# Attention's running maxima from row-packed scores: two half-array products of 64 rows in place of one of 96

## The reference, cut to what matters

```
scores = einsum('bhqd,bhkd->bhqk', q, k) / sqrt(16)      # masked by layer
attn   = softmax(scores)                                  # over the keys
out    = einsum('bhqk,bhkd->bhqd', attn, v)
```

## The kernel before, in words

| stage | max units | their matmuls, columns | score columns (L675, L678) | sum groups (L694) |
|---|---|---|---|---|
| layer 1, 8 tiles | 32 | 64, 25,616 | 26,624 | 26 |
| layer 2 | 48 | 106, 35,978 | 36,608 | 26 |
| layer 3 | 100 | 224, 90,144 | 92,160 | 58 |

## Time and profile before

### The profile page before, as it was taken

One profiled execution on the slowest core, in us unless ns is written; L12 is line 12 of the kernel. 1 busy time (PEld: TensorE's weight loads), 2 busy tenths in 40 slices (PEclk: granted clock), 3 DMA queues, 4 the chain that ended last, 5 costly groups with the idle time before them and its releaser, 6 DMA issues.

```text
span 5943.9 us, 71309 instructions
## 1 busy us (share of the span) xinstructions
PE 3795.9 (64%) x19888; PEld 1731.9 (29%) x19894; DVE 2791.6 (47%) x3817; ACT 1990.8 (33%) x3720; POOL 1506.2 (25%) x1461
## 2 busy tenths in 40 slices
PE   7700410037962013996599969974899999997695
PEld 2300200022321001332133336862222222222485
DVE  3131221276753276776566630013766666673201
ACT  1100100014751001673155621212366666664131
POOL 0767777677767400000000010010000000000202
PEclk9555655557986555998699979986799999999698
DMA  2331311013321211110211111534100111101243
GB/s 83 90 118 24 108 38 24 21 55 106 92 93 39 92 66 48 51 51 20 81 52 47 42 60 65 192 137 117 43 25 25 32 33 33 33 25 32 110 181 135
DMA packets 195461, 403.88 MB, mean 68 GB/s; under 512 B 46405, under 2 KB 130649, under 8 KB 186074
## 3 DMA queue, kind: packets, MB, share of 16 engines
q1 hardware_dynamic: 147114, 323.79, 17.0%
q0 software_dynamic: 48112, 77.16, 4.6%
HBM read 301.77 MB, written 106.10 MB: 69 GB/s over the span
## 4 chain that ended last, share of the span: by engine, by line
PE 47%; POOL 20%; DVE 10%; issue 10%; DMA 7%; ACT 2%; SPq 1%; POOLq 1%; DVEq 1%; ACTq 0%; PEldq 0%
POOL got_late L1319 13%; PE PS L694 13%; PE PS L657 9%; PE PS L675 8%; POOL s_got L1319 6%; PE PS L1959 5%; PE PS L1969 5%; DVE a_maxima L789 3%; ACT a_probs L745 1%; DMA q_parts<-a_parts 1%; PE PS L1929 1%; DMA late_rows<-got_late 1%; PE PS L1937 1%; PE PS L1122 1%; DMA Y<-denominators 1%
## 5 line engine op out<-in xcount | busy, mean ns | idle before, releaser
L789 DVE TENSOR_REDUCE a_maxima<-PS 128x1 f32<-128x1024 f32 (+8 forms) x1696 | 1637.9, 990 | 685.3 <-PE PS L657 468.7
L745 ACT ACTIVATE a_probs<-PS 128x512 f32<-128x512 f32 (+4 forms) x2896 | 1503.3, 572 | 771.7 <-PE PS L675 568.3
L657 PE MATMUL PS<-a_k_max,a_q_max 96*128 96x512 bf16 (+2 forms) x3136 | 913.5, 371 | 153.1 <-DVE a_maxima L789 90.4
L675 PE MATMUL PS<-a_q_exp,a_k_exp 97*128 97x512 bf16 (+4 forms) x2896 | 970.2, 376 | 58.6 <-ACT a_probs L745 30.6
L694 PE MATMUL PS<-a_probs,a_v_head 128*32 128x256 f32 (+4 forms) x7456 | 964.5, 496 | 31.8 <-DVE a_v_head L804 11.2
L2145 POOL IOTA e_slot_no<- 128x23 f32 x2 | 0.3, 162 | 2944.1 <-DVEq L2207 2944.1
L1319 POOL DMA_INDIRECT got_late<-kv_table,numbers x560 | 576.8, 1030 | 171.9 <-issue 171.9
L675 PEld LDWEIGHTS PS<-a_q_exp,a_k_exp 97*128 97x128 bf16 (+1 forms) x2896 | 271.7, 99 | 697.6 <-ACT a_probs L745 442.7
L657 PEld LDWEIGHTS PS<-a_k_max,a_q_max 96*128 96x128 bf16 x3136 | 263.8, 100 | 692.9 <-DVE a_maxima L789 386.6
L1319 POOL DMA_INDIRECT s_got<-kv_table,s_numbers x400 | 428.5, 1071 | 121.9 <-issue 121.9
L1298 PE MATMUL PS<-identity,s_ctx 128*128 128x128 f32 x18 | 6.2, 449 | 668.9 <-DVE s_ctx L1274 668.9
(11 more groups left out here) (342 smaller groups left out, 3309.9 us busy)
## 6 DMA issues: line engine op xcount, KB each, us to landing
e_w<-in_ew SPq DMA_DIRECT2D x41, 2052.0 KB, 8.1
late_rows<-got_late POOLq DMA_DIRECT2D x7, 2560.0 KB, 7.9
m_got<-late_rows SPq DMA_DIRECT2D x7, 2560.0 KB, 9.2
a_k_max<-k_parts SPq DMA_DIRECT2D x48, 300.2 KB, 3.8
a_k_exp<-k_parts SPq DMA_DIRECT2D x48, 300.2 KB
a_q_max<-q_parts SPq DMA_DIRECT2D x32, 384.0 KB, 3.6
a_q_exp<-q_parts SPq DMA_DIRECT2D x32, 384.0 KB
a_k_max<-k_parts SPq DMA_DIRECT2D x16, 684.2 KB, 5.7
```

Source lines behind the costliest of these rows:

```text
L657: last = pe.matmul(bank[:, b0:b1], q_max[hh][:, P * t:P * (t + 1)], k_max[hh][:, k0 + b0:k0 + b1], start=True, stop=not (lo < hi or masked))
L675: last = pe.matmul(bank[0:rows, q - CH * c:CH], k_exp[hh][:, k0:k0 + rows], q_exp[hh][:, q:CH * (c + 1)], start=True, stop=not (on_diag or ...
L745: act.activation(probs[i % PROB_SLOTS][0:rows, q - CH * c:CH], exp_bank[i % EXP_BANKS][0:rows, q - CH * c:CH], ACT.Exp).then_inc(probs_rea ...
L789: dve.tensor_reduce(maxima[hh][:, t, k0 // MAX_COLS:k0 // MAX_COLS + 1], max_bank[s[1] % MAX_SLOTS][:, 0:w], AX.X, ALU.max).then_inc(max_t ...
```

## The change

Four of the six groups of rows (64 rows) are used for the maxima. They stand first in DRAM, by a new order of the rows; the exponentials still use all 96. Two copies of the 64 query rows lie in partitions 0 to 63 and 64 to 127, and half of the keys beside each, so that a max unit is two matmuls of 64 rows, each in its own half of the array's rows and with its own PSUM bank. For causal keys the halves alternate every 256 keys. The diagonal's mask stays a matmul of 128 rows. Where the halves differ in width, VectorE makes two reductions of a unit. Layer 3's units don't cross from context to own keys any more. The row order now takes four stores for each piece in place of three, and `load_max` issues 4, 5 or 6 DMAs in place of two.

```diff
-QUERY_ROWS = ((0, 1, 2), (0, 1), (0,))
-KEY_ROWS = ((0, 0, 0), (1, 1), (2,))
+QUERY_ROWS = ((0, 1), (0, 1), (2,), (0,))
+KEY_ROWS = ((0, 0), (1, 1), (0,), (2,))
+HALF_ROWS = 4 * HD
+TURN = 256
+SPLIT_STORES = 16 * len(QUERY_ROWS)
...
+    sections = key_sections(n)
...
+                for c in range(0, lower, CH):
+                    wl, wu = min(CH, lower - c), max(0, min(CH, upper - c))
+                    max_steps.append(("max", len(max_units)))
+                    max_units.append((hh, t, at + c, wl, wu, slot, even, c, seen - P * t))
...
-                    for b0 in range(0, w, CH):
-                        b1 = min(b0 + CH, w)
-                        lo, hi = max(d0, k0 + b0), min(d1, k0 + b1)
-                        last = pe.matmul(bank[:, b0:b1], q_max[hh][:, P * t:P * (t + 1)], k_max[hh][:, k0 + b0:k0 + b1],
-                                         start=True, stop=not (lo < hi or masked))
...
+                    for half, w in enumerate((wl, wu)):
+                        if w:
+                            rows = slice(HALF_ROWS * half, HALF_ROWS * (half + 1))
+                            last = pe.matmul(bank[:, CH * half:CH * half + w], q_max[hh][rows, P * t:P * (t + 1)],
+                                             k_max[hh][rows, at:at + w], start=True,
+                                             stop=not (masked or (on_diag and d == half)))
+                    if on_diag:
+                        last = pe.matmul(bank[:, CH * d + d_at:CH * d + d_at + min(P, ahead)], env.mask_diag[:, :],
+                                         env.above_qk[:, 0:min(P, ahead)], start=False, stop=True)
...
-                    dve.tensor_reduce(maxima[hh][:, t, k0 // MAX_COLS:k0 // MAX_COLS + 1], max_bank[s[1] % MAX_SLOTS][:, 0:w],
-                                      AX.X, ALU.max).then_inc(max_taken, 1)
+                    if wu:
+                        taken = dve.tensor_reduce(maxima[hh][:, t, slot:slot + 1], bank.rearrange("p (b c) -> p b c", b=2)[:, :, 0:wu],
+                                                 AX.XY, ALU.max)
+                        slot += 1
+                    if wl > wu:
+                        taken = dve.tensor_reduce(maxima[hh][:, t, slot:slot + 1], bank[:, wu:wl], AX.X, ALU.max)
+                    taken.then_inc(max_taken, 1)
...
-            sp.dma_start(q_max[hh][:, :], head_rows(env.q_parts, h, T)).then_inc(q_max_in[hh], 16)
-            sp.dma_start(k_max[hh][:, :], head_rows(env.k_parts[n], h, keys)).then_inc(q_max_in[hh], 16)
+            whole = head_rows(env.k_parts[n], h, keys)
+            for half in range(2):
+                rows = slice(HALF_ROWS * half, HALF_ROWS * (half + 1))
+                sp.dma_start(q_max[hh][rows, :], head_rows(env.q_parts, h, T)[0:HALF_ROWS, :]).then_inc(q_max_in[hh], 16)
+                for even, at, base, length in sections:
+                    if even:
+                        w, first = (length + 1) // 2, base + (length - (length + 1) // 2) * half
+                        sp.dma_start(k_max[hh][rows, at:at + w], whole[0:HALF_ROWS, first:first + w]).then_inc(q_max_in[hh], 16)
+                        continue
...
+def key_sections(n):
+    even = (True, 0, 0, M)
+    return {1: [even], 2: [(False, 0, 0, M)], 3: [even, (False, (M + 3) // 4 * 2, M, S)]}[n]
+
+def half_columns(seen, half):
+    whole, rest = divmod(seen, 2 * TURN)
+    return TURN * whole + max(0, min(TURN, rest - TURN * half))
```

More of the change, by code:

```diff
@@ L337, in body @@
             act.wait_ge(projected, u + 1)
-            act.wait_ge(stored[k], turn * 48 + 48)
+            act.wait_ge(stored[k], turn * SPLIT_STORES + SPLIT_STORES)
             if bias is None:
@@ L526, in stage_attention @@
     last_chunk_tile = {c: max(t for t in range(KT) if tiles[t][2] < SUM * (c + 1)) for c in range(4)}
[L528 removed]
+    sections = key_sections(n)
+    max_units, max_steps, slots_per_tile = [], [], 0
     for hh in range(2):
         for t in range(nt):
[L531 to L536 removed]
+            slot = 0
+            for even, at, base, length in sections:
+                seen = length if even else min(length, P * (t + 1))
+                lower = (length + 1) // 2 if even else half_columns(seen, 0)
+                upper = lower if even else half_columns(seen, 1)
+                for c in range(0, lower, CH):
+                    wl, wu = min(CH, lower - c), max(0, min(CH, upper - c))
+                    max_steps.append(("max", len(max_units)))
+                    max_units.append((hh, t, at + c, wl, wu, slot, even, c, seen - P * t))
+                    slot += (wl > wu) + (wu > 0)
+            slots_per_tile = max(slots_per_tile, slot)
         max_steps.append(("row", hh))
[L538 removed]
     NE_, NM_, NS_ = len(exp_units), len(max_units), len(order)
@@ L556, in max_timeline @@
     def max_timeline(hh, span):
-        steps = [(max_units[s[1]][3] if s[0] == "max" else 0, s) for s in max_steps
+        steps = [(sum(max_units[s[1]][3:5]) if s[0] == "max" else 0, s) for s in max_steps
                  if (max_units[s[1]][0] if s[0] == "max" else s[1]) == hh]
@@ L590, in stage_attention @@
     first.close()
-    q_max = [sb(f"q_max{k}", [PARTS, T], bf16) for k in range(2)]
-    k_max = [sb(f"k_max{k}", [PARTS, keys], bf16) for k in range(2)]
+    q_max = [sb(f"q_max{k}", [2 * HALF_ROWS, T], bf16) for k in range(2)]
+    k_max = [sb(f"k_max{k}", [2 * HALF_ROWS, sections[-1][1] + (sections[-1][3] + 2 * TURN) // 2], bf16) for k in range(2)]
     q_exp = [sb(f"q_exp{k}", [PARTS + 1, T], bf16) for k in range(2)]
@@ new lines, in steps @@
+                    d = 0 if even else diagonal_half(t)
+                    d_at = 0 if even else diagonal_column(t) - c
+                    on_diag = not even and ahead > 0 and 0 <= d_at < (wl, wu)[d]
+                    for half, w in enumerate((wl, wu)):
[4 more added lines that the diff above has]
+                                             stop=not (masked or (on_diag and d == half)))
@@ new lines, in steps @@
+                    if on_diag:
+                        last = pe.matmul(bank[:, CH * d + d_at:CH * d + d_at + min(P, ahead)], env.mask_diag[:, :],
+                                         env.above_qk[:, 0:min(P, ahead)], start=False, stop=True)
+                    if masked:
+                        for half, w in enumerate((wl, wu)):
+                            k0 = c + (M - (M + 1) // 2) * half
+                            last = pe.matmul(bank[:, CH * half:CH * half + w], env.mask_diag[:, :], mask["qk"][:, t, k0:k0 + w],
```

37 lines of the change are left out of this document (18 added, 19 removed).

## The result

The changed kernel took 6559.05 us (median of 12 runs, 6550.21 to 6569.91), the kernel before on the same chip 6574.24 us (12 runs, 6571.14 to 6587.4). The ratio is 0.9978, 95% interval 0.997 to 0.9986: 15 us faster, just beyond what can be told from no change. The forecast was 6609, slower; the range held the time, the direction was wrong.

The account below looks back on a forecast made before the run. TensorE was taken to bound the attention loops; saved columns (-210 us), added shape changes (+218) and smaller terms summed to +34 on 6575, giving 6609 us, slower, with a range of 6470 to 6720.

Parts of the forecast that it names:

- Columns and changes of shape, taken together: In and after the attention loops: columns saved by halves streaming together, -210 us; added shape changes at 0.096 us each, +218.
- "faster" rival: Entering a 64-row half costs TensorE little: 6495 us at 0.046 a change, about 6390 at nothing; chance 0.27.
- Prologues: Ahead of the loops, halved matmuls hide behind VectorE's reductions: -5 us for each layer, -15 in all.
- Loads: At each stage's start the first max unit waits for 2, 3 or 4 more DMA issues: +3 us, between 0 and 8.
- VectorE in the loops: Added reductions hide in VectorE's free time; jitter makes TensorE's waits for VectorE a fifth longer: +8 us.
- A pair's own cost: Two weight loads ahead of the second half's columns, 0.02 us for each of 1,411 max units: +28, ends 0 and +280.
- Split stores: Four DMAs for three, same bytes: the added issue lengthens the split stages of the layers, +8 us, between 0 and 14.
- The clock: Full units gain at 1.2 GHz at layer 3's seam, -8 us; more frequent clock drops at layers 1 and 2's seams, +5.
- The statement about the span: Of the runs' median 6575.3 us, 631 lie around the profiled execution's span of 5943.9 and stay unchanged.
- Halves that don't stream together, or bare loads: Slower rival in the max units: 6820 us without overlap, 6750 with 0.1 us bare for each unit; bare loads' chance 0.10.
- The clock if half the rows are used: Slower rival: half-used rows don't hold 2.4 GHz, so matmuls take 0.43 us in place of 0.22: 6800 us; chance 0.07.

Follow-up runs that it names:

- half_columns: The kernel before with one full-array product over the first half of each max unit's columns, read twice by VectorE; ratio 0.9713 to the kernel before.
- VectorE halved: VectorE reads only half of each max unit: kernel before, ratio 0.9872; changed kernel, 0.9838; half_columns, 138.1 us an iteration of layer 3.
- VectorE and ScalarE halved: VectorE reduces and ScalarE takes exponentials of half the columns: kernel before, ratio 0.9831; half_columns, 0.944; changed kernel, 0.9776.
- after_again: The changed kernel, unedited, run again beside the kernel before on one chip: 6570.88 us against 6588.68, ratio 0.9978.
- four_stores: The kernel before with only the new order of its split rows, four stores for each piece in place of three; ratio 0.9998.
- same_rows: The changed kernel with both products of a max unit on rows 0 to 63, so nothing streams side by side; ratio 1.1051.
- grouping: The changed kernel with max units held back and placed together right behind or right ahead of sum groups; ratios to the kernel before 1.0411 and 1.0255.

## Why the prediction was wrong

**Terms that held.** *Columns and changes of shape, taken together*: in the loops the forecast had -199 and +207. With the other engines out of the way after is 7 x (-0.5 + 1.3 - 1.8) = -7 against before, and 7 x 1.2 = 8 of this is the seam of layer 3, so the two terms cancel as said. One by one they can be read cleanly in layer 1 only (5.1 for 5.3, and 4.6 for 4.7), where half_columns has just the columns of after. So the reading of the earlier trace rows was right, and my "faster" rival, a cheap change, wasn't how it became faster. *Prologues*: from the first maximum to the first exponential 28.3, 36.3 and 67.5 us became 23.9, 32.7 and 64.6, so -11 for -15. *Loads*: in layer 2 the first maximum came 7.0 us after the last split store landed, for 4.9 before: +2 there.

The Trainium skill ("TensorEngine Tiling (Array Packing)", Key Properties) has the drain on a change of mode, and the trace agrees with 0.10 us each way. The packing model of the Trainium skill ("TensorE: Matmul & The Clock Gate", Part 3: Packing small matmuls) has each further tile at about 4 ns, and the trace agrees with 3. Both are right at once; what decides is how often one leaves the mode.

**The step that failed.** It is the term *VectorE in the loops*, and behind it the way the sum was made. I took TensorE as the bound because it is busy 92 to 94% of the loops, added its terms in full, and gave its waits for VectorE one small extra (+8), as something that can only grow. The waits fell: from 4.7 to 0.9 us in an iteration of layer 3, 7 x -3.8 = -27 where +8 was forecast. That alone turns my +34 into about 0. The seams fell as well, by 1.2 us or -8 in seven iterations; my sum had no term for them, and why they are shorter stays open. That the range held the time is no merit of the sum: it was 250 us wide, and what it missed downward (the waits, the seams, the pairs, the stores) was in part made up by what it missed upward (the clock in layer 1).

How much of a term TensorE pays depends on its neighbours, as the three steps of relief show:

| layer 3, an iteration | half_columns less before | after less half_columns | after less before |
|---|---|---|---|
| by columns and changes of shape | -19.5 | +19.4 | 0 |
| nothing relieved | -12.0 | +6.6 | -5.4 |
| VectorE halved | -12.2 | +10.8 | -1.4 |
| VectorE and ScalarE halved | -17.6 | +15.8 | -1.8 |

VectorE's relief brings back 4 us of the second column (6.6 to 10.8) and nothing of the first; ScalarE's brings back 5 of either. 2 and 4 us don't come back. I read the fall of the wait so: the change of shape on entering a max unit is paid while the bank is still being read, and takes the place of a wait. There is another reading: a pair is done some 0.1 us sooner than two full matmuls (0.53 us after the start of the score ahead of it, for 0.65, by the distances of starts), so VectorE begins and frees the bank sooner. No run tells the two apart; the runs show that the waits went, and that TensorE's own work shows a gain of no more than 0.6 us once they and the seam are out.

**Terms that were mis-sized.** *A pair's own cost*: +28 forecast at 0.02 a unit; starts 0.003 apart make it +4. *Split stores*: +8 forecast, in the stages +3.9, -3.6 and -9.7, so -9. The issue was right, the landing not: I held the transfer's 6.8 us as fixed by its bytes. *The clock*: -8 and +5 forecast. The low stretch at layer 3's seam is 7.4 us, where before had 8.5 to 9.1; the -8 can't be read by itself. In layer 1's second half the low clock costs 2.7 us in an iteration that has it, all six in the first profile; in the second it costs 1.4 in two of six. In layer 2 it costs 1.4 in four and in three of six. That is +8 to +25 over seven iterations in place of +5, and layer 1's first half, which I had left out as hidden, comes on top.

Put together from the first profile of after: the loops 7 x (2.2 + 1.2 - 5.4) = -14, the prologues -11, the split stages -9, the loads +2, or some -32; its medians say -15. With the loops of after_again it is some -50, and its medians say -18. For after_again most of the difference can be found, because four_stores ran on the same chip. The last write of X comes 13.0 us later at the end of layer 1's first half (2597.2 for 2584.2), where five iterations take 44.4 us for 42.2; this half counts on such a chip. It comes 10.3 later at the end of the second half, 14.8 at that of layer 2, and 27.2 sooner at that of layer 3; the span is 24 us shorter. My terms give -50 + 13, less the -9 of the split stages that four_stores has too, so -28. The medians of the two are 17 us apart, since the profiled execution of after_again was 6 us under its median. What stays open is that the 9 us of the split stages don't show in four_stores, and the 17 us between -32 and -15 of the first session, which has no profile of before on its own chip.

**The statement about the span** was wrong, as said above, and with it the assumption that layer 1's first half is hidden by 180 us of gather: on the chips of the longer times it ends some 310 us after the gather. The sign that I passed over was the difference itself: a tenth of the time outside every instruction, for which nothing in the profile spoke.

**The rivals.** *Halves that don't stream together, or bare loads*: refuted by the starts. *The clock if half the rows are used*, at 0.07: it didn't happen to the change in that size. In same_rows a loop of half-array products ran at 0.55, beside 0.88 and 0.95 for the pairs; that the half rows are the reason is how I read it, and not shown.

## What to carry to other kernels

An engine that is busy 93% of a loop can still have a saving or a cost absorbed that is 5 to 8% of the loop (7.5 and 12.8 us of 155 here): before adding a cost and subtracting a saving of the same size, ask of each which wait it will fall into. A cost that is paid right where the engine waits anyway is cheap, and a saving there brings little. When two large terms cancel, the small waits listed for the bottleneck engine are the forecast, and they can fall as well as grow. An order of work in which fillers stand between dependent steps can be worth more than the switches it costs: saving 9 us of changes of shape by grouping brought in 38, of which 22 were waits. Finally, apply such a change stage by stage; here all of the gain was in layer 3, with its full units and long loop.

## What the runs showed of the hardware that was not expected

Products on half of the array's rows, one after another, did not hold the higher clock: layer 1's loop ran at 0.55 of full speed (1.2 GHz for 68 of 74 us an iteration) with TensorE 98% busy. The same products packed in pairs held 0.88 to 0.95 in that loop, and before held 0.95 with as many columns on 96 rows and fewer changes of shape. No run varied the number of rows alone, so what the chip counts stays open.

A transfer of the split rows landed 2 us sooner (4.72 for 6.76) when the same bytes went out as four stores in another order of rows, in place of three.

On two pairs of chips the same program differed by 10% (5953 and 5955 us, 6589 and 6592), all of it before layer 1's second half. The gather by GpSimd ended 230 us later, every other engine at times stood for some 30 us with nothing in the profile that it waited for, and layer 1's first half, hidden on the one kind, ran mostly after the gather. Each chip was used in one session only, so the runs don't tell a property of the chip from one of the session.
